# 24 row buffers in the first edge pass of a four-layer graph network, and lookup differences made by TensorE and ScalarE

## The chip, the cores and the metric

The kernel runs on one core of a Trainium2 chip. The metric is the device time of one execution in microseconds (us), smaller is better. The kernel before takes 4315.98 us (median of three runs, 4315.5 to 4325.66).

## The reference, cut to what matters

Four graph layers run one after another over 6250 nodes of 128 features and 100000 edges sorted by destination. The change lies in the first one, an attention layer:

```python
h = jnp.maximum(_layernorm(x, axis=-1), 0.0)
# L0: x + attention(h)
h = x @ W                      # x is the normed h above
a_s = h @ att_src
a_d = h @ att_dst
e = leaky_relu(a_s[src] + a_d[dst], 0.2)
m = segment_max(e, dst)
p = exp(e - m[dst])
denom = segment_sum(p, dst)
out = segment_sum(h[src] * (p / denom[dst])[:, None], dst) + bias
```

Self loops are added to the edges. The sum over edges is taken of the normed rows, and W is applied to the sums per node.

## The kernel before, in words

Nodes are padded to 6656 (52 blocks of 128, 13 groups of 512), edges to 784 tiles of 128, which make 98 chunks of C = 8 tiles. Each phase is a block in which every engine has its own program, and a barrier stands between blocks. The phases of the first layer, with their times in the profiled execution:

- Norm (0 to 43 us): writes the normed rows to the table in HBM and, turned, to `m.hT` in SBUF.
- Setup (`setup_phase`, 43 to 66 us): SyncE loads five index arrays, VectorE splits each source number into its place in a block (`lo`, 7 bits, stored to `lo_dram`) and its block (`m.src_hi`), and makes other constants.
- Tables (`attention_tables_phase`, 66 to 107 us): products of `m.hT` give a_s and a_d; a_s goes through `as_dram`.
- Lookup (`lookup_phase`, 107 to 272 us): finds a_s[src] for every edge, 49 steps of 16 tiles. A step n loads `place` (SyncE, 512 KB, four buffers), compares it with the partition's number (VectorE, `onehot`, L534), multiplies it by a_s in three bf16 parts (PE, 48 products, L559), and takes the entry of the right block: GpSimd subtracts the source's block from the numbers 0 to 51 (`away`, L520), VectorE keeps the product where `away` is zero (`masked`, L540) and sums it up (L546). `onehot`, `away`, `masked` and the PSUM tile have two buffers each.
- Maxima (`segment_max_phase`, 272 to 306 us): scans over the edges on VectorE.
- Edge pass (`attention_edges`, 306 to 1163 us): for each chunk VectorE makes the weights from onehots and ScalarE's exp (`weigh`), PE adds weighted rows and weights into PSUM (L1216, L1217, after a 384-column clear, L788), and VectorE adds them to the accumulator (`add`).
- Output (`attention_output`, from 1163 us): products of the sums and of `m.hT` with W, x loaded again and added.

The rows of the sources are gathered from the table by GpSimd, one indirect DMA of 128 rows (64 KB) for each of the 784 tiles. Since the table stands after the norm, gathers start early: `gather_straight` issues 14 in setup, 30 in tables, one per lookup step, 20 in the maxima, and then what is missing to the ring's end. The ring has RING0 = 16 buffers of 8 tiles, so 128 tiles: `m.rows` (4 buffers) and `m.more` (12). From then on `gather_long_ring` (L838 is the DMA in its helper) waits for `rows_free` of the buffer, and for marks in VectorE's chain. VectorE's loop over chunks has 8 chunks in a turn (SHARED), those of PE and ScalarE have as many as the ring.

## Time and profile before

| what | us |
|---|---|
| median of three runs | 4315.98 |
| the profiled execution | 4312.96 |
| its span, first to last instruction | 4311.2 |
| edge pass of the first layer within it | 306 to 1163 |
| lookup within it | 107 to 272 |

| engine | busy us | share |
|---|---|---|
| PE (matmul) | 3632.9 | 84% |
| PEld (weight load) | 3011.9 | 70% |
| GpSimd | 2880.6 | 67% |
| VectorE | 2142.4 | 50% |
| ScalarE | 1362.6 | 32% |

The shares are averages over four layers with different limits, so they say little about one phase. What matters is read per stage: who is busy, and whom the engine waits for that ends the stage. In the views, "idle before <-releaser" is the time an engine stood still just before an instruction, and what ended it; "issue" is time in which it waited for nothing that the profile shows.

### The profile page before, as it was taken

Reading aid. Unit: us, or ns where it says so; the run is one execution under the profiler, and the core shown is the slowest. Engines: PE = TensorE matmul, PEld = TensorE weight load, DVE = VectorE, ACT = ScalarE, POOL = GpSimd, SP = SyncE. Lnnn points to the kernel's source line nnn. Section 1 sums busy time; section 2 is a strip of 40 time slices with the busy share of each in tenths; the row PEclk is TensorE's granted clock in tenths of the full one; section 3 lists DMA queues with packets and bytes.
Section 4 is the critical chain, followed back from the end, with each engine's and each line's share of the span. In section 5 each row is a group of like instructions: output and inputs, shape, how many; then the busy total and the mean of one; then the engine's idle time right before and its main releaser. Section 6 shows DMA issues by size and latency. Waiting matters only on the chain. (4 is left out here: it accounts for less than half of the span.)

```text
span 4311.2 us, 76764 instructions
## 1 busy us (share of the span) xinstructions
PE 3632.9 (84%) x20596; PEld 3011.9 (70%) x20597; DVE 2142.4 (50%) x6554; ACT 1362.6 (32%) x1910; POOL 2880.6 (67%) x2980
## 2 busy tenths in 40 slices
PE   3649999777678999999998868888888865999997
PEld 1649999767647888888887845555565643777775
DVE  4874444433375555555555744444444446444442
ACT  2000000000051111111113756666666655444442
POOL 4877777777536777777761057777777764777772
PEclk9555555555585555555557978777777775999998
DMA  4632222222263333333322133333333333111122
GB/s 116 200 122 52 53 53 54 53 53 53 71 234 87 79 79 80 77 79 79 79 71 87 51 113 108 105 100 105 100 105 101 104 81 86 52 51 51 50 51 53
DMA packets 257318, 364.29 MB, mean 85 GB/s; under 512 B 53022, under 2 KB 179413, under 8 KB 256981
## 3 DMA queue, kind: packets, MB, share of 16 engines
q0 software_dynamic: 90624, 185.78, 17.0%
q1 hardware_dynamic: 166489, 176.37, 13.3%
q14 instruction: 148, 1.21, 0.1%
q8 instruction: 57, 0.93, 0.1%
HBM read 319.53 MB, written 42.41 MB: 84 GB/s over the span
## 5 line engine op out<-in xcount | busy, mean ns | idle before, releaser
L838 POOL DMA_INDIRECT m_rows<-table,e_idx x1112 | 1065.1, 958 | 350.2 <-issue 291.9
L838 POOL DMA_INDIRECT e_rows<-table,e_idx x480 | 463.2, 965 | 144.7 <-issue 142.6
L838 POOL DMA_INDIRECT m_more<-table,e_idx x480 | 454.0, 946 | 145.6 <-issue 120.4
L1217 PE MATMUL e_agg<-e_weights,m_ones 128*128 128x32 f32 x1568 | 481.6, 401 | 0.0
L838 POOL DMA_INDIRECT m_hT<-table,e_idx x416 | 393.1, 945 | 125.7 <-issue 103.3
L1217 PEld LDWEIGHTS e_agg<-e_weights,m_ones 128*128 128x128 f32 x1568 | 428.3, 333 | 0.0
L1654 PE MATMUL e_z<-e_edge,e_w 128*128 128x512 f32 x392 | 268.3, 822 | 167.2 <-DVEq L1735 153.9
L1216 PE MATMUL e_agg<-e_weights,m_more 128*128 128x16 f32 x1152 | 339.7, 375 | 79.2 <-issue 64.5
L1216 PEld LDWEIGHTS e_agg<-e_weights,m_more 128*128 128x128 f32 x1152 | 311.4, 330 | 105.0 <-issue 105.0
L1543 PE MATMUL e_out<-e_counts,e_nodes 128*128 128x256 bf16 x2964 | 383.2, 280 | 0.0
L1883 PE MATMUL e_x<-e_key,e_rows_T 128*128 x1568 | 373.7, 420 | 2.5 <-DMA e_key<-key_dram 2.5
L1385 ACT ACTIVATE e_counts<-e_count 128x832 bf16<-128x832 f32 x304 | 262.8, 865 | 319.4 <-PE e_count L1536 319.4
L1883 PEld LDWEIGHTS e_x<-e_key,e_rows_T 128*128 128x128 f32 x1568 | 352.5, 330 | 9.5 <-issue 7.6
L1543 PEld LDWEIGHTS e_out<-e_counts,e_nodes 128*128 128x128 bf16 x2964 | 297.8, 101 | 79.5 <-issue 6.2
L1665 PEld LDWEIGHTS e_z<-e_w,e_filt 128*128 128x128 f32 x1568 | 254.2, 254 | 49.0 <-issue 49.0
L1665 PE MATMUL e_z<-e_w,e_filt 128*128 128x128 f32 x1568 | 278.5, 350 | 0.0
L1142 ACT ACTIVATE e_pl<-e_diff 128x8 f32<-128x8 f32 x98 | 20.6, 210 | 802.0 <-DVE e_diff L1176 802.0
L1654 PEld LDWEIGHTS e_z<-e_edge,e_w 128*128 128x128 f32 x392 | 88.3, 250 | 258.1 <-DVEq L1735 157.8
L1844 ACT ACTIVATE e_p<-e_p 128x32 f32<-128x32 f32 x98 | 22.5, 229 | 685.6 <-DVEq L2012 685.6
L1676 PE MATMUL e_agg<-e_onehot,e_message 128*128 128x16 f32 x1568 | 222.1, 285 | 13.2 <-DVE e_message L1747 13.2
L1907 PEld LDWEIGHTS e_agg<-e_weights,m_hT 128*128 128x128 f32 x928 | 199.0, 326 | 42.6 <-issue 42.6
L1676 PEld LDWEIGHTS e_agg<-e_onehot,e_message 128*128 128x128 f32 x1568 | 212.4, 217 | 21.2 <-issue 13.6
(318 smaller groups left out, 6766.2 us busy)
## 6 DMA issues: line engine op xcount, KB each, us to landing
e_edge<-edge_T SPq DMA_DIRECT2D x98, 512.0 KB
lu_place<-lo_dram SPq DMA_DIRECT2D x49, 512.0 KB, 3.8
e_key<-key_dram SPq DMA_DIRECT2D x98, 256.0 KB
m_rows<-table,e_idx POOLq DMA_INDIRECT x1152, 2.6
key_dram<-key_out SPq DMA_DIRECT2D x13, 1024.0 KB, 4.7
table<-m_rows SPq DMA_DIRECT2D x39, 256.0 KB, 2.4
e_rows<-table,e_idx POOLq DMA_INDIRECT x528, 2.6
m_more<-table,e_idx POOLq DMA_INDIRECT x480, 2.5
```

The costliest lines, as they stand in the source:

```text
L838: pool.indirect_dma_start(rows[:, t, :], None, table, bass.IndirectOffsetOnAxis(ap=idx[:, t:t + 1], axis=0)).then_inc(landed[t * len(lande ...
L1142: act.activation(pl[b][:, :, 0], diff[:], ACT.Exp).then_inc(p_ready, 1)
L1216: pe.matmul(to[:, 0, cols], s.rows[at.r][:, t, :], both[:, t, 0, :], start=False, stop=False)
L1217: ins = pe.matmul(to[:, 1:3, cols], m.ones[:], both[:, t, :, :], start=False, stop=(t == C - 1))
L1385: act.activation(counts[at.b][:, :, t * W_NARROW:(t + 1) * W_NARROW].rearrange("p (h n) w -> p h n w", h=2), count_ps[t % 2][:, :, 0:PART] ...
L1543: ins = pe.matmul(out_ps[b][:, 0:L * W_NARROW], nodes[:, part, block_no, :], counts[b][:, block_no, :], start=(i == 0), stop=(i == 3 * NB ...
L1654: ins = pe.matmul(z1[:, cols], w1[:], edge[at.b][:, cols], start=True, stop=True)
L1665: ins = pe.matmul(z2[at.b][:, cols], filt1[at.b][:, cols], w2[:], start=False, stop=(t % G4 == G4 - 1))
L1676: ins = pe.matmul(agg[at.b][:, ds(rel[t], W)], message[at.b][:, t * P:(t + 1) * P], s.onehot[at.b][:, t * W:(t + 1) * W], start=False, sto ...
L1844: act.activation(p[:], p[:], ACT.Exp).then_inc(p_ready, 1)
L1883: ins = pe.matmul(to[:, q * HEADS * W:(q + 1) * HEADS * W], rows_T[:, t, :], key[at.b][:, :, ds(rel[t], W)], start=True, stop=True)
L1907: ins = pe.matmul(to[:, :, ds(rel[t], W)], s.rows[at.r][:, t, :], part[:, q * HEADS * W:(q + 1) * HEADS * W], start=False, stop=(t == C - 1))
```

## The change

The ring of the first edge pass gets 24 buffers: four in `m.rows`, 14 in `m.more` and six (`OVER_HT`) over the first 6144 columns of `m.hT`. For this, the tables phase stores these columns to `hT_dram` in four DMAs of SyncE (`hT_kept`, waited for by GpSimd ahead of tile 128), and the output phase loads them back in four DMAs of ScalarE's queue (`hT_loaded`, waited for by PE's products). The last two buffers of the ring lie in `m.more` and hold `away` during the lookup. The ring's `rows_free` counts are written out for a turn of 24, and each buffer has one semaphore for its eight gathers, not two.

In the lookup, GpSimd no longer makes `away`. PE makes it in two products of 17 rows by 416 columns a step (a row of ones times 0 to 51, less the source's block, from `hi_T`), and ScalarE copies it from PSUM to SBUF. GpSimd issues 17 gathers in 8 steps, not 8 (`lookup_gathers`: 104 in 49 steps, not 49), so 168 tiles are gathered or under way when the edge pass begins, not 113. In setup the load of `src_el` goes, and the block numbers are made from the other array, stored as bf16 (`hi_dram`) and loaded once at the start of the lookup.

```diff
-RING0 = 16
+RING0 = 24
+OVER_HT = 6
...
+def lookup_gathers(step):
+
+    return step * 17 // 8
...
-                sp.dma_start(hi_i[:], k.dram["src_el"]).then_inc(loaded, 16)
...
-                sp.wait_ge(stored, 16)
-                sp.wait_ge(loaded, 80)
+                sp.wait_ge(hi_ready, 1)
+                sp.dma_start(k.dram["hi_dram"].rearrange("(p t) -> p t", p=P), hi_b[:]).then_inc(stored, 16)
+                sp.wait_ge(stored, 32)
+                sp.wait_ge(loaded, 64)
...
-                v.wait_ge(loaded, 80)
...
+                v.wait_ge(loaded, 64)
+
+                ch.step(v.tensor_scalar(hi_i[:], lo_i[:], 7, None, ALU.logical_shift_right))
+                v.tensor_copy(hi_b[:], hi_i[:]).then_inc(hi_ready, 1)
                 ch.step(v.tensor_scalar(lo_i[:], lo_i[:], P - 1, None, ALU.bitwise_and))
                 v.tensor_copy(lo_b[:], lo_i[:]).then_inc(lo_ready, 1)
-                ch.step(v.tensor_scalar(hi_i[:], hi_i[:], 7, None, ALU.logical_shift_right))
-                ch.add(v.tensor_copy(m.src_hi[:], hi_i[:]))
...
                 sp.dma_start(wT[:], k.dram["W0T"]).then_inc(loaded, 16)
...
+                over = OVER_HT * C * P // 4
+                for n in range(4):
+                    sp.dma_start(k.dram["hT_dram"][:, n * over:(n + 1) * over], m.hT[:, n * over:(n + 1) * over]
+                                 ).then_inc(early.hT_kept, 16)
                 sp.wait_ge(copied, NG)
                 sp.dma_start(k.dram["as_dram"].unsqueeze(0), row[:]).then_inc(moved, 16)
                 sp.wait_ge(moved, 16)
...
-        away, masked = [sb(f"away{b}", [P, L, NB], F32) for b in range(2)], [sb(f"masked{b}", [P, L, NB], F32) for b in range(2)]
-        block_ps = [ctx.enter_context(nc.psum_tensor(f"lu_ps{b}", [P, L, PER], F32)) for b in range(2)]
+        masked = [sb(f"masked{b}", [P, L, NB], F32) for b in range(2)]
+        last_rows = (RING0 - RING - OVER_HT - 2) * C * P
+        away = [m.more[:, last_rows + b * L * NB:last_rows + (b + 1) * L * NB].rearrange("p (l n) -> p l n", n=NB) for b in range(2)]
+        assert 2 * L * NB <= 2 * C * P and IN_SETUP + IN_TABLES + lookup_gathers(T // L) <= (RING0 - 2) * C
+        hi_T, away_of = sb("hi_T", [L + 1, T // L, P], BF16), sb("away_of", [L + 1, L, NB], BF16)
+        block_ps, away_ps = [[ctx.enter_context(nc.psum_tensor(f"lu_{n}{b}", [P, L, PER], F32)) for b in range(2)] for n in ("ps", "away")]
...
+        parts = [steps * n // 4 for n in range(5)]
...
+                sp.dma_start(hi_T[1:L + 1, :, :], k.dram["hi_dram"].rearrange("(n t p) -> t n p", t=L, p=P)).then_inc(hi_loaded, 16)
                 for t, d in ((m.dst_here, "dst_el"), (m.dst_beside[:, 0, :], "dst_before"), (m.dst_beside[:, 1, :], "dst_after")):
...
             def _(pool):
                 pool.sem_inc(masked_ready, 2)
...
                     pool.wait_ge(masked_ready, n + 1)
-                    pool.tensor_tensor(away[n % 2][:], m.iota_f[:, 0:NB].unsqueeze(1).to_broadcast([P, L, NB]),
-                                       m.src_hi[:, n * L:(n + 1) * L].unsqueeze(2).to_broadcast([P, L, NB]),
-                                       ALU.subtract).then_inc(away_ready, 1)
-                    gather_straight(pool, k, m, early, k.table[0], IN_SETUP + IN_TABLES + n, 1)
+                    gather_straight(pool, k, m, early, k.table[0], IN_SETUP + IN_TABLES + lookup_gathers(n),
+                                    lookup_gathers(n + 1) - lookup_gathers(n))
...
+            @block.scalar
+            def _(act):
+                for n in range(4):
+                    part = hi_T[0:1, parts[n]:parts[n + 1], :].rearrange("p n d -> p (n d)")
+                    act.activation(part, m.ones[0:1, 0:1].to_broadcast([1, part.shape[1]]), ACT.Copy).then_inc(ones_ready, 1)
+
+                def take(at):
+                    act.wait_ge(numbers_ready, at.n + 1)
+                    act.wait_ge(masked_ready, at.n + 1)
+                    act.activation(away[at.b], away_ps[at.b][:, :, 0:NB], ACT.Copy).then_inc(away_ready, 1)
+                skewed(act, steps, Item, [(0, take)])
...
+                v.tensor_scalar(away_of[:], m.ident[0:L + 1, 1:L + 1].unsqueeze(2).to_broadcast([L + 1, L, NB]), -1.0, None,
+                                ALU.mult).then_inc(away_of_ready, 1)
+                v.wait_ge(away_of_ready, 1)
+                v.tensor_copy(away_of[0:1, :, :], m.iota_f[0:1, 0:NB].unsqueeze(1).to_broadcast([1, L, NB])).then_inc(away_of_ready, 1)
...
-                    v.wait_ge(away_ready, at.n + 1)
+                    v.wait_ge(away_ready, at.n + 3)
...
                 def product(at):
+                    pe.wait_ge(away_ready, at.n + 1)
+                    for half in range(2):
+                        tiles = slice(half * L // 2, (half + 1) * L // 2)
+                        ins = pe.matmul(away_ps[at.b][:, tiles, 0:NB], hi_T[:, ds(at.n, 1), :].rearrange("k n p -> k (n p)"), away_of[:, tiles, :],
+                                        start=True, stop=True)
+                    ins.then_inc(numbers_ready, 1)
                     pe.wait_ge(onehot_ready, at.n + 1)
                     pe.wait_ge(masked_ready, at.n + 1)
                     for q in range(L):
@@ -559,6 +598,10 @@
                             ins = pe.matmul(block_ps[at.b][:, q, 0:NB], onehot[at.b][:, q * P:(q + 1) * P],
                                             m.as_part[:, part, :], start=(part == 0), stop=(part == 2))
...
+                pe.wait_ge(hi_loaded, 16)
+                pe.wait_ge(away_of_ready, 2)
+                pe.wait_ge(ones_ready, 4)
+                pe.sem_inc(away_ready, 2)
                 skewed(pe, steps, Item, [(0, product)])
...
-                gather_straight(pool, k, m, early, k.table[0], IN_SETUP + IN_TABLES + T // (2 * C), IN_MAXIMA)
+                gather_straight(pool, k, m, early, k.table[0], IN_SETUP + IN_TABLES + lookup_gathers(T // (2 * C)), IN_MAXIMA)
...
-    early.gathered = [[nc.alloc_semaphore(f"{name}gathered{r}_{q}") for q in range(2)] for r in range(len(rows))]
+    early.gathered = [[nc.alloc_semaphore(f"{name}gathered{r}")] for r in range(len(rows))]
...
 def gather_straight(pool, k, m, early, table, first, count):
...
+    over_hT = (RING0 - OVER_HT - 2) * C
     for n in range(first, min(first + count, len(early.rows) * C)):
+        if n == over_hT:
+            pool.wait_ge(early.hT_kept, 64)
         pool.indirect_dma_start(early.rows[n // C][:, n % C, :], None, table,
-                                bass.IndirectOffsetOnAxis(ap=m.src_idx[:, n:n + 1], axis=0)).then_inc(early.gathered[n // C][n % C // (C // 2)], 16)
+                                bass.IndirectOffsetOnAxis(ap=m.src_idx[:, n:n + 1], axis=0)).then_inc(early.gathered[n // C][0], 16)
...
-            pool.wait_ge(s.rows_free[r % shared], turn * (ring // shared) + r // shared)
+            pool.wait_ge(s.rows_free[r % shared], (turn - 1) * (ring // shared) + (r // shared + 2))
...
+        over = OVER_HT * C * P // 4
+        hT_loaded = [a.sem(f"hT_loaded{n}") for n in range(4)]
...
                 def products(g):
                     if g >= 3:
                         pe.wait_ge(y_free, g - 2)
+                    if g * GN < 4 * over:
+                        pe.wait_ge(hT_loaded[g * GN // over], 16)
                     for kind, rows in enumerate((acc[:, 0, :], m.hT[:])):
...
             @block.scalar
             def _(act):
+                for n in range(4):
+                    cols = slice(n * over, (n + 1) * over)
+                    act.dma_start(m.hT[:, cols], k.dram["hT_dram"][:, cols]).then_inc(hT_loaded[n], 16)
                 act.wait_ge(shifted, 1)
...
-            m.more = sbuf(layer, "more", [P, (RING0 - RING) * C * P])
-            rows_of = lambda n: m.more[:, n * C * P:(n + 1) * C * P].rearrange("p (t d) -> p t d", d=P)
-            early = early_rows(nc, "g0_", [rows[:] for rows in m.rows] + [rows_of(n) for n in range(RING0 - RING)],
-                               IN_SETUP + IN_TABLES + k.T // (2 * C) + IN_MAXIMA)
+            own = RING0 - RING - OVER_HT
+            m.more = sbuf(layer, "more", [P, own * C * P])
+            rows_of = lambda t, n: t[:, n * C * P:(n + 1) * C * P].rearrange("p (t d) -> p t d", d=P)
+            early = early_rows(nc, "g0_", [rows[:] for rows in m.rows] + [rows_of(m.more, n) for n in range(own - 2)] +
+                               [rows_of(m.hT, n) for n in range(OVER_HT)] + [rows_of(m.more, n) for n in (own - 2, own - 1)],
+                               IN_SETUP + IN_TABLES + lookup_gathers(k.T // (2 * C)) + IN_MAXIMA)
```

## Rows read from the trace of the kernel before

**Rows 1.** By stage: busy us of each engine (instructions), PEclk, DMA share, GB/s

```profile
400.00:500.00 100.00, 97.58 (x437) 92.38 (x437) 46.62 (x250) 4.13 (x15) 75.75 (x82) 0.50 0.21 53
...
900.00:1000.00 100.00, 74.59 (x330) 69.99 (x330) 35.62 (x191) 3.38 (x11) 75.75 (x82) 0.50 0.21 53
```

**Rows 2.** Timeline (start us, us, engine, operation, [idle <-releaser]): gathers

```profile
306.88 0.95 POOL L877 DMA_INDIRECT m_more<-table,m_src_idx  x1 [5.32 <-SPq L1128]
...
328.24 0.97 POOL L838 DMA_INDIRECT m_rows<-table,e_idx  x1 [2.63 <-DVEq L1195]
...
1148.11 0.94 POOL L838 DMA_INDIRECT m_rows<-table,e_idx  x1 [0.30 <-issue]
```

**Rows 3.** Costliest group on GpSimd, 40 to 1160 us

```profile
L838 POOL DMA_INDIRECT m_more<-table,e_idx x480 | 454.0, 946 | 145.6 <-issue 120.4 <-DVE e_masked L1169 7.9 <-DVE e_ade L1171 4.9
```

**Rows 4.** Whom PE waited for (us, times, longest): 400 to 780, 820 to 1140

```profile
PE e_agg L1216 <- DVEq L1185: 14.3, 6, 2.8
...
PE e_agg L1216 <- issue: 72.5, 28, 2.9
```

**Rows 5.** Timeline: chunks 9 and 57 on ScalarE, 57 and 97 on PE

```profile
387.22 0.21 ACT L1142 ACTIVATE e_pl<-e_diff 128x8 f32<-128x8 f32 x1 [11.76 <-DVE e_diff L1176]
...
756.80 0.21 ACT L1142 ACTIVATE e_pl<-e_diff 128x8 f32<-128x8 f32 x1 [12.21 <-DVE e_diff L1176]
...
757.92 0.60 PE L1216 MATMUL e_agg<-e_weights,m_more 128*128 128x16 f32 x2 [2.83 <-DVEq L1185]
...
1152.34 0.60 PE L1216 MATMUL e_agg<-e_weights,m_rows 128*128 128x16 f32 x2 [4.03 <-issue]
```

**Rows 6.** Timeline: one step of the lookup on all engines

```profile
201.96 1.58 POOL L520 TENSOR_TENSOR lu_away<-m_iota_f,m_src_hi 128x832 f32<-128x832 f32 x1 [0.18 <-DVE lu_masked L540]
...
202.04 1.02 DVE L546 TENSOR_REDUCE m_s_el<-lu_masked 128x832 f32 x1 [0.16 <-DVE lu_masked L540]
...
202.97 1.11 DVE L534 TENSOR_SCALAR lu_onehot<-lu_place,m_part_f 128x2048 bf16<-128x2048 bf16 x1
...
203.69 1.24 POOL L877 DMA_INDIRECT m_more<-table,m_src_idx  x1
...
204.01 1.01 DVE L540 SCALAR_TENSOR_TENSOR lu_masked<-lu_away,lu_ps 128x832 f32<-128x832 f32 x1
...
204.15 2.26 PE L559 MATMUL lu_ps<-m_as_part,lu_onehot 128*128 128x52 bf16 x48 [0.88 <-DVE lu_onehot L534]
...
205.10 1.58 POOL L520 TENSOR_TENSOR lu_away<-m_iota_f,m_src_hi 128x832 f32<-128x832 f32 x1 [0.18 <-DVE lu_masked L540]
```

**Rows 7.** Timeline: a onehot of the lookup with GpSimd idle

```profile
117.94 0.75 DVE L534 TENSOR_SCALAR lu_onehot<-lu_place,m_part_f 128x2048 bf16<-128x2048 bf16 x1 [1.13 <-DMA lu_place<-lo_dram]
```

**Rows 8.** Timeline: a scan and the gather begun inside it

```profile
275.32 1.79 DVE L646 TENSOR_TENSOR_SCAN sg_run<-sg_bars,m_s_el 128x784 f32<-128x784 f32 x1
...
275.81 2.06 POOL L877 DMA_INDIRECT m_more<-table,m_src_idx  x1 [0.30 <-issue]
```

**Rows 9.** Groups by form: 384-column product, ScalarE copy of 832

```profile
L788 PE MATMUL e_agg<-m_zeros 1*128 1x384 bf16 x62 | 30.8, 496 | 0.0
...
L1385 ACT ACTIVATE e_counts<-e_count 128x832 bf16<-128x832 f32 x304 | 262.8, 865 | 319.4 <-PE e_count L1536 319.4
```

**Rows 10.** Timeline: first operation of the setup on VectorE

```profile
53.06 0.57 DVE L150 TENSOR_SCALAR su_lo<-su_lo 128x784 int32<-128x784 int32 x1 [10.97 <-DMA su_hi<-src_el]
```

**Rows 11.** Timeline: the last store of the tables phase

```profile
99.31 0.29 SPq L430 DMA_DIRECT2D as_dram<-at_row  x1
```

**Rows 12.** Timeline of the output phase, and its busy time by stage

```profile
1168.60 6.59 SPq L210 DMA_DIRECT2D m_more<-x_in  x4
...
1168.85 2.08 PE L2142 MATMUL o_y<-o_w,m_acc 128*128 128x128 f32 x8 [9.48 <-DMA o_lines<-as_dram]
...
1177.23 15.76 POOL L226 TENSOR_TENSOR m_more<-m_more,o_bias 128x512 f32<-128x512 f32 x11 [28.18 <-DVE o_share L2187]
...
1168.00:1182.00 14.00, 8.45 (x52) 7.94 (x52) 6.44 (x15) 3.61 (x13) 4.77 (x4) 0.74 0.96 250
```

More of the change, by code:

```diff
@@ L118, in setup_phase @@
         hi_i = sb("su_hi", [P, T], I32)
+        hi_b = sb("su_hib", [P, T], BF16)
         span = sb("su_span", [P, 2, T], F32)
@@ L122, in setup_phase @@
         loaded = sem("su_loaded")
-        lo_ready = sem("su_lo_ready")
+        lo_ready, hi_ready = sem("su_lo_ready"), sem("su_hi_ready")
         chain = sem("su_chain")
@@ L494, in lookup_phase @@
         onehot = [sb(f"onehot{b}", [P, L * P], BF16) for b in range(2)]
-        away, masked = [sb(f"away{b}", [P, L, NB], F32) for b in range(2)], [sb(f"masked{b}", [P, L, NB], F32) for b in range(2)]
-        block_ps = [ctx.enter_context(nc.psum_tensor(f"lu_ps{b}", [P, L, PER], F32)) for b in range(2)]
+        masked = [sb(f"masked{b}", [P, L, NB], F32) for b in range(2)]
[4 more added lines that the diff above has]
+        block_ps, away_ps = [[ctx.enter_context(nc.psum_tensor(f"lu_{n}{b}", [P, L, PER], F32)) for b in range(2)] for n in ("ps", "away")]
         place_ready, place_free = [sem(f"place_ready{r}") for r in range(4)], sem("place_free")
-        onehot_ready, block_ready, away_ready = sem("onehot_ready"), sem("block_ready"), sem("away_ready")
+        onehot_ready, block_ready = sem("onehot_ready"), sem("block_ready")
+        hi_loaded, ones_ready, away_of_ready = sem("hi_loaded"), sem("ones_ready"), sem("away_of_ready")
+        numbers_ready, away_ready = sem("numbers_ready"), sem("away_ready")
         masked_ready, picked = sem("masked_ready"), sem("picked")
@@ L537, in pick @@
                     v.wait_ge(block_ready, at.n + 3)
-                    v.wait_ge(away_ready, at.n + 1)
+                    v.wait_ge(away_ready, at.n + 3)
                     v.wait_ge(picked, at.n + 1)
-                    v.scalar_tensor_tensor(masked[at.b][:], away[at.b][:], 0.0, block_ps[at.b][:, :, 0:NB], ALU.is_equal, ALU.mult).then_inc(masked_ready, 1)
+                    v.scalar_tensor_tensor(masked[at.b][:], away[at.b], 0.0, block_ps[at.b][:, :, 0:NB], ALU.is_equal, ALU.mult).then_inc(masked_ready, 1)
                     v.wait_ge(onehot_ready, at.n + 1)
@@ L866, in early_rows @@
     early.rows, early.begun = rows, begun
-    early.gathered = [[nc.alloc_semaphore(f"{name}gathered{r}_{q}") for q in range(2)] for r in range(len(rows))]
+    early.gathered = [[nc.alloc_semaphore(f"{name}gathered{r}")] for r in range(len(rows))]
     early.idx_loaded, early.dst_loaded = nc.alloc_semaphore(name + "idx_loaded"), nc.alloc_semaphore(name + "dst_loaded")
-    early.all = sum(early.gathered, []) + [early.idx_loaded, early.dst_loaded]
+    early.hT_kept = nc.alloc_semaphore(name + "hT_kept")
+    early.all = sum(early.gathered, []) + [early.idx_loaded, early.dst_loaded, early.hT_kept]
     return early
 def gather_straight(pool, k, m, early, table, first, count):
+    over_hT = (RING0 - OVER_HT - 2) * C
     for n in range(first, min(first + count, len(early.rows) * C)):
+        if n == over_hT:
+            pool.wait_ge(early.hT_kept, 64)
         pool.indirect_dma_start(early.rows[n // C][:, n % C, :], None, table,
-                                bass.IndirectOffsetOnAxis(ap=m.src_idx[:, n:n + 1], axis=0)).then_inc(early.gathered[n // C][n % C // (C // 2)], 16)
+                                bass.IndirectOffsetOnAxis(ap=m.src_idx[:, n:n + 1], axis=0)).then_inc(early.gathered[n // C][0], 16)
 def first_turn(pool, k, m, early, table):
@@ L2769, in build @@
                     norm_phase(nc, k, m, "n0_", k.table[0], x_from=k.dram["x_in"], early=early, measured=False)
-                m.src_hi, m.as_part = sbuf(first, "src_hi", [P, k.T]), sbuf(first, "as_part", [P, 3, k.NB], BF16)
+                m.as_part = sbuf(first, "as_part", [P, 3, k.NB], BF16)
                 with ExitStack() as su:
```

4 lines of the change are left out of this document (2 added, 2 removed).

## The prediction

> **What bounds the kernel now.** I went from the stages to the waits, then to single instructions. By stage, the first edge pass has two halves: from 400 to 500 us PE is busy 97.58 of 100 us, from 900 to 1000 only 74.59, while GpSimd stands at 75.6 to 75.8 in both [rows 1]. GpSimd's 75.7% is a full engine: a gather takes 0.946 us, and 0.30 us of idle time follows each (145.6 us over 480) [rows 3]. That makes 1.249 us a tile, 9.99 us a chunk of eight. On the timeline it never pauses: the first gather of the pass starts at 306.88, the first of the loop at 328.24, where it waited 2.63 us for a freed buffer, and the last at 1148.11 [rows 2]. Over 306.88 to 1148.11 stand 671 gathers, the 784 tiles less the 113 before the pass; 670 distances of 1.249 are 836.8 us, the wait and six index copies make up the remaining 4.4 of the 841.2.
>
> PE's waits say the same. From 400 to 780 us it waits only for VectorE's weights, 14.3 us in all; from 820 to 1140 it has 72.5 us in 28 waits at "issue", one ahead of each chunk's products, where the rows aren't there yet [rows 4]. PE lives on the stock of 128 tiles until about 795 us and then walks behind GpSimd. Its own pace is seen on ScalarE's exp, one per chunk: chunk 9 at 387.22, chunk 57 at 756.80 [rows 5], so 369.58 / 48 = 7.70 us a chunk. The pass ends by GpSimd: last gather out at 1149.05, PE starts chunk 97 at 1152.34 [rows 5], 7 us of products, the sums added, and the output phase opens at 1163.6.
>
> GpSimd's whole work is 784 × 1.249 = 979 us from 43 us on, plus what it does besides: 49 differences of 1.58 us. What shortens this layer is each gather that moves from the pass into time in which GpSimd doesn't gather now.
>
> **The change part by part.** *Edge pass.* 168 tiles are issued before it, not 113: 55 gathers fewer, 55 × 1.249 = 68.7 us. With 24 buffers GpSimd goes straight on for 24 gathers (30 us); chunk 0 is freed about 21 us into the pass, as now (wait ended at 328.24, pass began at 306), so the 2.63 us wait goes as well. The marks ask for chunk c - 22 to be weighed; VectorE is there first, now and then. A little longer index copies (192 columns, not 128) cost below 0.5 us. GpSimd's end comes 68.7 + 2.6 - 0.3 = **71.0 us** earlier, and chunk 97 could start at 1081.3.
>
> What is late next is PE. It starts chunk 57 at 757.92 [rows 5]; forty chunks at 7.70 later is 1065.9. So PE is 15 us ahead of GpSimd at the end, catching up with it around chunk 90, and the whole 71.0 counts. It takes 0.16 us more per chunk (15 / 98) before PE binds. The unrolled loops of PE and ScalarE grow from 16 to 24 chunks, which the trace can't price: between a little below 0 (fewer turns) and the 2.83 us that PE waits at a turn of VectorE's loop [rows 5], four times, 11 us. Even this fits into the 15. One semaphore instead of two per buffer changes neither, as PE needs all eight tiles anyway.
>
> *Lookup.* The period of a step is 3.14 us: GpSimd's difference starts at 201.96 and 205.10, and VectorE is full: 1.11 (onehot), 1.01 (masked), 1.02 (sum) [rows 6]. GpSimd is as full, with 1.58 and a gather of 1.24. The onehot takes 0.75 us while GpSimd stands still [rows 7], and 1.11 in this step: it ends at 204.08, 0.54 us after GpSimd's difference (203.54), so it waits for that. Without the difference VectorE needs 0.75 + 1.01 + 1.02 less 0.1 of overlap, 2.7; gathers may hold it up a little, so 2.7 to 3.0. PE now does 48 products in 2.26 us and waits 0.88 for the onehot [rows 6]. It gets two products of 416 columns. Bounds: by the stream of 52-column products, 2.26 / 48 = 0.047 us each or 0.905 ns a column, 2 × 0.38 = 0.75 us; by the lone 384-column product at 0.496 [rows 9], 2 × 0.53 = 1.06 us. They stand ahead of the wait for the onehot, so they fill the 0.88: 2.26 + 0.75 is 3.01, + 1.06 is 3.32. I take 3.05, near the stream, because weights and products follow each other there without a gap. ScalarE's copy of 832 PSUM columns is 0.865 [rows 9], under a 3 us step, and it is over before the 48 products are. GpSimd has 2.125 × 1.249 = 2.65 us a step, 2.95 if each step has one gather stretched by 0.30 as now (1.24 against 0.946), and nobody waits for it inside the phase. So 49 × (3.14 - 3.05) = 4.4 us less. At the start `hi_T` (200 KB in runs of 256 B) goes ahead of the first `place`, about 1 us at the 250 GB/s of [rows 12], and up to 3; the ones (6272 columns on ScalarE, 6.5 us by the 0.865 for 832) and `away_of` (two VectorE operations of 1 us) lie under the wait for the first `place`, 9 us from the phase's start at 107 to the onehot before that of [rows 7]. Lookup: **-3.4 us**, bounds -20 (2.7 a step) to +12 (3.32 a step and 3 us).
>
> *Setup.* VectorE starts at 53.06, when the last of five loads is in [rows 10]. It had stood idle for 10.97 us, so a fifth of the bytes, 401 KB, is at most 2.2 us; the number of VectorE's operations stays. I take **-1.5**, bounds 0 and -2.2. *Tables.* 3.1 MB of stores enter SyncE's queue behind the small loads at 67 us and ahead of the store of a_s at 99.31 [rows 11]. At the 250 GB/s of [rows 12] they are through by 80, so nothing: 19 us of cover. Were it gone, the a_s chain would shift by what is left of them. GpSimd's wait for `hT_kept` stands at tile 128, in the lookup, over 100 us later: nothing.
>
> *Output.* ScalarE's queue loads 3.1 MB from 1164 on. Ahead of the first products stand SyncE's small loads (PE starts at 1168.85), then x is loaded from 1168.60, and GpSimd begins to use it at 1177.23 [rows 12]. The queue moves 250 GB/s in this stretch [rows 12]: 3.1 MB is 12.6 us, 6.5 MB is 26 us from 1164, to 1190. GpSimd adds the bias to 11 groups in 15.76 us, so it asks for the last slab of x (group 9) at 1190, and PE, three groups ahead at most, for the last quarter of `m.hT` no earlier than 1186. So most is covered; the two small round trips ahead of 1173 share the engines with bulk. **+2 us**, bounds 0 and +8.
>
> Sum: -71.0 - 3.4 - 1.5 + 2 = **-73.9 us**. On the profiled execution 4312.96 - 73.9 = 4239.1; this execution lies 3 us below the median of the three runs, so against the median 4315.98 - 73.9 = **4242**.
>
> **Where the Trainium skill speaks against this.** A gather begun inside a VectorE scan takes 2.06 us, not 0.95: the scan started at 275.32 with 1.79 us, and the gather comes out 0.76 us after the scan's end [rows 8]. The Trainium skill, "SBUF — State Buffer", section "SBUF: two separate sides", says that VectorE and GpSimd share one pair of ports under an exclusive lock, and that a GpSimd DMA's descriptors can't be written while VectorE runs in a two-port mode. The trace agrees in kind. By that rule a onehot may shut a gather out for up to its whole length in each step, which is rival A below.
>
> **The rivals.** *A: gathers and onehots collide.* If each of the 2.125 gathers per step is stretched, by 0.30 as now, GpSimd needs 3.29 us a step; with one stretched by 0.75 it is 3.40. Then the lookup ends by GpSimd and costs 49 × 0.2 = 10 us rather than saving 4. For it: the stretched gather is there now. Against: gathers then start at any point of the step, not always inside a onehot. With PE's products at their upper bound the time is about the same: 4242 + 3.4 + 12 = **4257**.
>
> *B: PE runs at its other level in the lookup.* The granted clock is 0.50 (1.2 GHz) in both stretches of the edge pass, even at 97.58% busy [rows 1], and PE in the lookup goes from 72 to some 97% busy. If the clock rose to 1.0, PE's products halve, VectorE alone sets 2.8 a step, and 49 × 0.34 = 17 us are saved, less 1: **4230**. The row of the edge pass speaks against it. The Trainium skill, "TensorE: Matmul & The Clock Gate", section "Part 1: The HAM clock gate", says that the throttled state is the default and sustained activity releases it; that would favour B, but the 97.58% row doesn't agree.
>
> *C: PE is the bound of the pass.* Longer loops or later weights take the chunk to 8.0 us: 40 × 0.3 = 12 behind chunk 57, 17 over the first 57, 29 in all, less the 15 of slack: +14, **4256**. The 16-chunk loops show no stall of PE or GpSimd at their turns, only VectorE's at its 8; against it.
>
> *D: the lookup becomes one chain, the other sign.* `away` now passes PE, ScalarE and VectorE, and PE's wait for `away_ready` stands ahead of the 48 products. If the two buffers don't decouple this, a step is 0.75 + 0.87 + 2.26 + 1.01 and four handovers of some 0.1, 5.3 us: 49 × 2.16 = 106 us more, 4242 + 3.4 + 106 = **4351**, slower. It decides from 3.14 + 71 / 49 = 4.6 us a step. Against it: PE needs only step n - 2's copy, which is over for two whole steps; VectorE needs step n's copy, made under the 48 products.
>
> **How the numbers follow.** Forecast 0.66, range of its own 4232 to 4252 (2.9 to 3.15 a step in the lookup, output 0 to +6, a few us from other layers). A 0.13, B 0.09, C 0.07, D 0.03, and 0.02 for another cause with no gain. The likeliest gives 4242. The range that leaves out D and the tails goes from 4226 to 4263. About 0.3% (13 us) is what a measurement of this kernel can tell from no change; all cases but D and the last are far faster. Faster 0.95, same 0.02, slower 0.03.
>
> **What would show it.** Right: 616 gathers from the start of the edge pass, still 1.249 apart, GpSimd without a wait; PE over 95% busy until near chunk 90 and few waits at "issue" after; the last gather about 71 us nearer to the pass's start. In the lookup, steps of 3.0 to 3.1 us, onehots near 0.8, PE nearly full. Output phase as long as before within 3 us. Wrong would be: PE waiting between chunks in the middle of the pass; a gather waiting for `rows_free`; the pass ended by PE; lookup steps over 3.3; x or `m.hT` late in the output phase, seen as PE's wait for a DMA.

## The result, and the profile after

The kernel after takes 4261.7 us (median of four runs, 4253.4 to 4266.2), the kernel before 4318.7 beside it: ratio 0.9863, 95% interval 0.9851 to 0.9876, so 57 us less by the medians, where 74 were forecast. The profiled execution took 4266.2 us, its span 4263.1; it was the slowest of its four, so the two profiles lie only 46.8 us apart (48.4 by their spans). Phase by phase they differ so:

| phase | forecast | profiles |
|---|---|---|
| setup and tables | -1.5 | -2.0 |
| lookup | -3.4 | -2.8 |
| edge pass, first to last gather | -71.0 | -66.0 |
| output phase | +2 | +8.5 |
| norm and key phases of layer 2 | 0 | +2.9 |
| layer 2's pass | 0 | +6.9 |
| all behind it | 0 | +4.6 |

By stage [rows 1]: PE is now as busy from 900 to 1000 us as it used to be in the first half only, GpSimd at 75.7 as before, and the granted clock stays at 0.50 (1.2 GHz).

```profile
400.00:500.00 100.00, 97.14 (x435) 91.88 (x435) 44.95 (x241) 4.01 (x14) 75.78 (x80) 0.50 0.20 54
900.00:1000.00 100.00, 93.46 (x417) 88.13 (x417) 44.91 (x244) 2.73 (x13) 75.73 (x80) 0.50 0.19 53
```

The gathers of the pass, by the buffer they fill [rows 3]. The mean of one is 951 to 955 ns, not 946:

```profile
L881 POOL DMA_INDIRECT m_more<-table,e_idx x336 | 320.7, 955 | 102.0 <-issue 82.6 <-DVE e_masked L1216 7.0 <-DVE e_weights L1229 4.0
L881 POOL DMA_INDIRECT m_hT<-table,e_idx x144 | 137.0, 951 | 43.9 <-issue 36.0 <-DVE e_onehot L1145 1.8 <-DVE e_masked L1216 1.5
```

Whom PE waited for [rows 4], from 400 to 780 us and from 820 to 1070. The 72.5 us at "issue" are gone; what is left at the end is nine waits for the rows of late chunks (23.1 us; two of the three buffers are shown):

```profile
PE e_agg L1263 <- DVEq L1232: 11.9, 6, 2.3
...
PE e_agg L1263 <- DMA m_hT<-table,e_idx: 15.1, 6, 2.9
PE e_agg L1263 <- DMA m_more<-table,e_idx: 5.3, 2, 2.7
```

The lookup on the timeline [rows 6], first a step with PE at 1.2 GHz, then one at 2.4:

```profile
199.67 0.74 DVE L567 TENSOR_SCALAR lu_onehot<-lu_place,m_part_f 128x2048 bf16<-128x2048 bf16 x1
199.91 0.87 PE L591 MATMUL lu_away<-lu_away_of,lu_hi_T 17*128 17x416 bf16 x2
200.04 1.20 POOL L924 DMA_INDIRECT m_more<-table,m_src_idx  x1 [0.30 <-issue]
...
200.72 2.26 PE L598 MATMUL lu_ps<-m_as_part,lu_onehot 128*128 128x52 bf16 x48
200.82 0.86 ACT L551 ACTIVATE m_more<-lu_away 128x832 f32<-128x832 f32 x1 [3.10 <-PE lu_away L591]
201.48 1.02 DVE L579 TENSOR_REDUCE m_s_el<-lu_masked 128x832 f32 x1
...
204.28 1.02 DVE L579 TENSOR_REDUCE m_s_el<-lu_masked 128x832 f32 x1 [0.16 <-DVE lu_masked L573]
...
205.22 0.52 PE L591 MATMUL lu_away<-lu_away_of,lu_hi_T 17*128 17x416 bf16 x2
...
206.02 1.40 PE L598 MATMUL lu_ps<-m_as_part,lu_onehot 128*128 128x52 bf16 x48 [0.28 <-DVE lu_onehot L567]
...
207.03 1.02 DVE L579 TENSOR_REDUCE m_s_el<-lu_masked 128x832 f32 x1
```

The sums (L579) follow each other after 2.80 and 2.75 us, not 3.14. By this VectorE's part of the lookup, from the phase's start (107.2 before, 105.2 now) to its last sum, went from 164 to 149 us. But the phase is only 2.8 us shorter, and its end shows why:

```profile
253.04 1.02 DVE L579 TENSOR_REDUCE m_s_el<-lu_masked 128x16 f32<-128x832 f32 x1
...
257.51 0.95 POOL L924 DMA_INDIRECT m_hT<-table,m_src_idx  x1 [0.30 <-issue]
267.23 0.33 SPq L641 DMA_DIRECT2D el_dram<-m_s_el  x1
...
267.88 1.21 POOL L924 DMA_INDIRECT m_hT<-table,m_src_idx  x1 [9.42 <-POOLq L522]
```

VectorE is done at 254.1. GpSimd's last gather is out at 258.5, and then nothing is seen for 8.5 us, until the barrier opens at 267.1. GpSimd's program has one drain at the end of each block, the instruction behind which the engine joins the barrier (shortest, median, longest in ns, then when it starts):

```profile
L522 POOLq DRAIN  x1: 18576/18576/18576, 248.4 to 248.4; - x1
```

It ends at 248.4 + 18.6 = 267.0. Nothing else works in the last 6.5 us of it, and no data moves (by stage, the columns of [rows 1]):

```profile
260.50:267.00 6.50, 0.00 (x0) 0.00 (x0) 0.00 (x0) 0.00 (x0) 0.00 (x0) 0.50 0.00 0
```

Before, with 49 gathers in the block, it ended at 264.8 + 7.1 = 271.8, which is 4.1 us past the last gather, and the phase ended 0.6 us after VectorE:

```profile
L503 POOLq DRAIN  x1: 7059/7059/7059, 264.8 to 264.8; - x1
```

The opening of the output phase [rows 12], first two lines of before that the rows do not have, then after:

```profile
1163.64 0.53 SPq L2113 DMA_DIRECT2D line_dram<-m_acc  x2
1175.42 0.29 ACT L2156 ACTIVATE o_e<-o_e 128x104 f32<-128x104 f32 x1 [32.61 <-DVEq L2181]
```

```profile
1092.30 0.54 SPq L2162 DMA_DIRECT2D line_dram<-m_acc  x2
1092.31 2.73 ACTq L2208 DMA_DIRECT2D m_hT<-hT_dram  x4
...
1099.73 0.34 SPq L2167 DMA_DIRECT2D o_lines<-line_dram  x1
1100.11 11.07 SPq L218 DMA_DIRECT2D m_more<-x_in  x4
1105.97 2.08 PE L2193 MATMUL o_y<-o_w,m_acc 128*128 128x128 f32 x8 [17.92 <-DMA o_lines<-as_dram]
...
1112.55 0.29 ACT L2210 ACTIVATE o_e<-o_e 128x104 f32<-128x104 f32 x1 [41.53 <-DVEq L2235]
```

PE's first product comes 13.7 us after the start of the phase, where it was 5.2 (1168.85 less 1163.64), behind SyncE's small load `o_lines`, which was issued at 1094.96 and shares the DMA engines with 3.1 MB issued at 1092.31. ScalarE's exp stands 20.3 us after the start, 11.8 before. From there to ScalarE's last scaled product both kernels take the same 36.5 us.

### The profile page after: what moved, and what is told of

It reads as the page before. It is cut to its first block and busy times, and to the rows that moved or that the text cites. A ratio compares the mean times of both kernels' runs of the same rounds, so it can differ in the third digit from the quotient of the medians.

```text
span 4263.1 us, 76891 instructions
## 1 busy us (share of the span) xinstructions
PE 3642.8 (85%) x20694; PEld 3005.7 (71%) x20695; DVE 2123.1 (50%) x6556; ACT 1407.9 (33%) x1961; POOL 2813.3 (66%) x2929
## 5 line engine op out<-in xcount | busy, mean ns | idle before, releaser
L881 POOL DMA_INDIRECT m_rows<-table,e_idx x1048 | 1006.8, 961 | 329.1 <-issue 291.6
L881 POOL DMA_INDIRECT m_hT<-table,e_idx x560 | 535.0, 955 | 169.6 <-issue 143.2
L881 POOL DMA_INDIRECT m_more<-table,e_idx x336 | 320.7, 955 | 102.0 <-issue 82.6
L1263 PE MATMUL e_agg<-e_weights,m_more 128*128 128x16 f32 x896 | 264.3, 375 | 13.5 <-DVEq L1232 8.2
L1263 PEld LDWEIGHTS e_agg<-e_weights,m_more 128*128 128x128 f32 x896 | 242.2, 330 | 32.4 <-issue 32.4
L1189 ACT ACTIVATE e_pl<-e_diff 128x8 f32<-128x8 f32 x98 | 20.6, 210 | 738.3 <-DVE e_diff L1223 738.3
```

The lines of the kernel that those rows point to most:

```text
L881: pool.indirect_dma_start(rows[:, t, :], None, table, bass.IndirectOffsetOnAxis(ap=idx[:, t:t + 1], axis=0)).then_inc(landed[t * len(lande ...
L1263: pe.matmul(to[:, 0, cols], s.rows[at.r][:, t, :], both[:, t, 0, :], start=False, stop=False)
```

## The experiments

**e1: the kernel before once more.**

> The kernel before, unchanged, with a second profile. In the first two profiles a gather of the first edge pass follows the last after 1.249 us before the change and 1.256 us after it (616 x 0.007 = 4 us), and layers 2 to 4 take 14 us longer after the change, though no line of them differs. Theory 'execution': both are differences of one profiled execution from the next; then this profile's pitch may be either one, and layers 2 to 4 differ from the first profile's by several us. Rival 'kernel': the change causes both (for instance because GpSimd runs no tensor operation in the lookup); then this profile shows 1.249 us again and every phase within 1.5 us of the first one.

4315.1 us, 0.9996 (0.9987 to 1.0006). The gathers of the pass have the pitch and the mean time (946 ns) of the first profile, and layer 2's pass, from the first to the last of ScalarE's 196 operations at L1839, lasts 967.4 us (966.6). But layers 3 and 4 together end 5.9 us earlier than in the first profile with nothing changed: so much of a difference of two profiles means nothing there. What differs in layer 2's pass can be read, what differs in layers 3 and 4 can't.

**e2, e3, e4: the change taken apart.** e2 has the ring, its store and its reload alone; e3 also the new lookup, with one gather a step; e4 has the ring and 104 gathers, with GpSimd making the differences.

```diff
 def lookup_gathers(step):
-    return step * 17 // 8
+    return step
```

(e2 and e3; in e2 and e4 the functions of the lookup and the setup are those of before, the gathers of a step counted by `lookup_gathers`.)

> The ring of 24 buffers with six over m.hT, its store in the tables phase and its load in the output phase, but the lookup and the setup as before: GpSimd makes the differences and issues 49 gathers there, so 113 tiles stand before the pass. Theory 'gathers moved': the ring alone takes away GpSimd's wait of 2.63 us for a freed buffer, and the reload in the output phase costs 8.9 us as in the changed kernel's profile: +6 us against before. Rival 'output cost is due to the earlier phases, not to the reload': -3 us. Rival 'a larger ring helps by itself': below -10 us.

> The changed kernel with one gather per lookup step (49, not 104). Theory 'GpSimd ends the changed lookup': the lookup phase of the changed kernel ended at 267.2 by GpSimd, whose last gather was over at 258.5 and whose drain lasted until 267.0, while VectorE was done at 254.2. With 49 gathers GpSimd keeps pace and its drain is near 4 us as before, so the phase ends near 255 to 257, 16 us earlier than before the change. The pass then has 671 gathers again and takes as long as before less 2.6 us; with +9 in the output phase the whole comes to -5 to -12 us against before. Rival 'the drain belongs to the new lookup, not to the number of gathers': the phase ends near 263 or later, and the whole is 0 to +5 us against before. If the prediction's sum were right (55 gathers are worth 71 us in the pass and cost nothing in the lookup), the whole would be 4242 + 71 = 4313, -3.

> The changed kernel with GpSimd making the differences again, as before, but with the 104 gathers in the lookup. Theory 'GpSimd is the resource': a step of the lookup becomes 1.58 (difference) + 2.125 x 1.25 + 0.2 to 0.5 = 4.4 to 4.7 us instead of 3.14, +62 to +77 us in the lookup and about 4 us more of drain; the pass saves 71 and the output costs 9: +4 to +19 us against before. So the move of the difference to TensorE and ScalarE would be what the gain is made of. Rival 'GpSimd has room': the step stays below 3.6 us and the whole is -35 us or better.

| ratio to before | 49 gathers in the lookup | 104 gathers |
|---|---|---|
| differences by GpSimd | e2: 1.0017 (1.0007 to 1.0026) | e4: 1.0005 (0.9996 to 1.0015) |
| differences by PE and ScalarE | e3: 0.9991 (0.9982 to 1.0001) | after: 0.9863 (0.9851 to 0.9876) |

Against e2, each half alone is worth 0.1 to 0.3% (5 to 11 us), both together 1.5% (66 us). The ring costs 6 us by itself, as expected: its output phase is 8.2 us longer than before, its edge pass 1.0 us shorter.

e4's step is 4.26 us, a little under what was expected:

```profile
203.14 2.24 DVE L545 TENSOR_SCALAR lu_onehot<-lu_place,m_part_f 128x2048 bf16<-128x2048 bf16 x1
203.23 1.60 POOL L530 TENSOR_TENSOR lu_away<-m_iota_f,m_src_hi 128x832 f32<-128x832 f32 x1
204.99 1.24 POOL L892 DMA_INDIRECT m_more<-table,m_src_idx  x1 [0.16 <-issue]
...
206.53 0.94 POOL L892 DMA_INDIRECT m_more<-table,m_src_idx  x1 [0.30 <-issue]
207.40 2.25 DVE L545 TENSOR_SCALAR lu_onehot<-lu_place,m_part_f 128x2048 bf16<-128x2048 bf16 x1
```

The onehot takes 2.24 us where it takes 0.74 otherwise: it begins 0.09 us ahead of GpSimd's difference and ends 0.55 after it, so it stood still for nearly the whole of it. The pass starts 63.4 us later than before, and the 55 gathers give back 69. Against before e4 lost 2 us by the ratio (-2 to +6), where 4 to 19 were expected.

For e3 the lookup was expected to end at 255 to 257; it ends at 251.8, with VectorE:

```profile
246.03 0.95 POOL L924 DMA_INDIRECT m_more<-table,m_src_idx  x1 [1.80 <-DVE lu_masked L573]
...
250.43 1.02 DVE L579 TENSOR_REDUCE m_s_el<-lu_masked 128x16 f32<-128x832 f32 x1
...
252.58 1.21 POOL L924 DMA_INDIRECT m_more<-table,m_src_idx  x1 [5.60 <-POOLq L522]
```

```profile
L522 POOLq DRAIN  x1: 5232/5232/5232, 245.8 to 245.8; - x1
```

The drain is over at 251.0, 4.1 us after the last gather. In e4, with 104 gathers and the old lookup, it is 8.5 us. So in this phase it goes with the number of gathers (49: 4.1, 104: 8.5), not with the kernel. The pass starts 20.6 us earlier than before; of the gain of the 55 gathers (69 us) the changed kernel pays 15 in its lookup. By the whole time e3 gained 4 us, a little less than the 5 to 12 expected, since its pass is 4.3 us longer than before and layer 2's 8.3 us (the gather time, below).

**e5 to e8: on another chip.** In these runs the kernel before took 5542 us.

> The changed kernel, unchanged, as the base for the three below and with a second profile. In e1, e2 and e4 (GpSimd makes the differences) a gather takes 0.94 us and has a pitch of 1.25 from the lookup on to the end of layer 3, and layer 2's pass lasts 966 to 967 us; in the changed kernel and in e3 (TensorE makes them) the gather takes 0.95 with a pitch of 1.26 through layers 1 and 2, and layer 2's pass lasts 974 to 975. Theory 'kernel': this profile repeats 1.26 and 974 (within 1), and the whole is 54 to 60 us below before. Rival 'execution': 1.25 and 966 turn up.

> The changed kernel, but GpSimd doesn't wait for VectorE's step before it issues the gathers of the lookup: 104 of them back to back. In the changed kernel it stands still from 110.7 to 120.6, its last gather is out at 258.5, and its drain ends the phase at 267.0, though VectorE is done at 254.2. Theory 'GpSimd's drain grows with the gathers and ends the phase': the last gather is out near 106 + 104 x 1.33 = 244, the drain of 8.5 us is over at 253, the phase ends with VectorE near 255, and the whole is 12 us (10 to 13) below the changed kernel. Rival 'the drain starts to count only when the phase's other work ends': the phase ends at 263 or later, -4 us at most. Rival 'gathers without pacing collide with VectorE's onehots and the loads of place': VectorE's last step moves past 258, -8 us at most.

> The changed kernel, but in the output phase ScalarE waits until the small line loads are in before it issues the 3.1 MB of m.hT, and TensorE turns the lines ahead of its first product. The opening of the output phase (its start to ScalarE's exp) was 11.8 us before the change and 20.4 after. Theory 'the bulk load stands in the way of the small ones': the opening falls to 11 to 13 us, and the whole by 6 to 9 us below the changed kernel. Rival 'the bytes cost what they cost': m.hT and x come in later instead, PE or GpSimd waits for a DMA further on, and the whole gains less than 3 us.

> The changed kernel with a single GpSimd subtraction more (128 x 208, result unused) at the start of the lookup. Theory 'a tensor operation on GpSimd sets how long the later gathers take': from there the gather takes 0.94 us with a pitch of 1.25, 4 us less in the first edge pass and 7 us less in layer 2's: -11 us against the changed kernel (-8 to -13). Rival 'it isn't the operation' (place of the code, or something else of the old lookup): 0.95 and 1.26 as in the changed kernel, 0 within 2 us.

e6 takes one line away, e7 adds one and moves the transposes, e8 adds one operation:

```diff
                 for n in range(steps):
-                    pool.wait_ge(masked_ready, n + 1)
                     gather_straight(...)
```

```diff
-                products(0)
                 pe.wait_ge(lines_loaded, 64)
...
-                for g in range(1, NG):
+                for g in range(NG):
...
             def _(act):
+                act.wait_ge(lines_loaded, 64)
                 for n in range(4):
```

```diff
+                pool.tensor_tensor(spare[:], m.iota_f[:, 0:NB]..., m.part_f[:]..., ALU.subtract)
```

Against before on the same chip: e5 (the changed kernel) 1.0025 (1.0006 to 1.0043), e6 1.0146 (1.0118 to 1.0174), e7 1.0024 (1.0006 to 1.0041), e8 0.9999 (0.9978 to 1.0020). On this chip the change brings nothing (at best 0.06% slower by its interval), and gathers back to back in the lookup cost 75 us more. The timelines of PE and GpSimd in e6:

```profile
160.61 0.20 PE L597 MATMUL lu_ps<-m_as_part,lu_onehot 128*128 128x52 bf16 x1 [1.90 <-issue]
163.41 0.20 PE L597 MATMUL lu_ps<-m_as_part,lu_onehot 128*128 128x52 bf16 x1 [2.60 <-issue]
166.21 0.20 PE L597 MATMUL lu_ps<-m_as_part,lu_onehot 128*128 128x52 bf16 x1 [2.60 <-issue]
```

```profile
162.28 0.95 POOL L923 DMA_INDIRECT m_more<-table,m_src_idx  x1 [0.30 <-issue]
163.54 0.95 POOL L923 DMA_INDIRECT m_more<-table,m_src_idx  x1 [0.30 <-issue]
```

The gathers keep their pitch, and every other engine stands at "issue": PE shows a product every 2.8 us where 48 took 2.26, and from 160 to 240 us it is busy for 6.4 us, VectorE for 2.7. In e5 VectorE had 60.4 us of "issue" ahead of `e_weights` in the edge pass. There a gather isn't free for the engines beside it, and work moved beside it is paid for. What differs in that chip no trace here shows. The times of these four don't answer the questions they were made for; e6 and e7 were run again. e8's gathers don't bear out its theory either: they kept the long time through the first layer (median 958 ns) and took the short one (947) from layer 2 on.

**e9 and e10, on the first chip.**

> The kernel of e6 once more, since e5 to e8 ran on a chip on which the kernel before took 5542 us, and VectorE and TensorE started an instruction only every 1.4 to 2.7 us while GpSimd gathered. On a chip where before takes about 4318 us: theory 'the drain grows with the gathers and ends the phase': last gather out near 244, drain over near 253, phase over with VectorE near 255, ratio to before 0.9863 - 0.0028 = 0.9835 (0.982 to 0.985). Rival 'the drain counts only from the end of the phase's other work': phase over at 263 or later, 0.9855 or more. Rival 'back-to-back gathers hold the other engines up in the lookup here too, as in e6': the steps of the lookup stretch, phase over after 270, ratio 0.988 or more.

> The kernel of e7 once more, on a chip where before takes about 4318 us. Theory 'the bulk load stands in the way of the small ones': from the start of the output phase to ScalarE's exp 11 to 13 us, not 20.4; ratio to before 0.9863 - 0.0018 = 0.9845 (0.983 to 0.986). Rival 'the bytes cost what they cost': a wait for m.hT or x later in the phase gives it back, and the phase is less than 3 us shorter than in the changed kernel (0.9856 or more).

e9: 4248.9 us, 0.9849 (0.9833 to 0.9866). That is 13 us below the changed kernel by medians but 6 by the ratios to the kernel before beside each, and the two intervals overlap, so the gain is read from the phase. Its lookup ends at 256.8, 10.3 us earlier:

```profile
246.88 1.27 POOL L923 DMA_INDIRECT m_hT<-table,m_src_idx  x1 [0.30 <-issue]
...
250.27 1.02 DVE L578 TENSOR_REDUCE m_s_el<-lu_masked 128x16 f32<-128x832 f32 x1
256.92 0.33 SPq L640 DMA_DIRECT2D el_dram<-m_s_el  x1
```

```profile
L522 POOLq DRAIN  x1: 25117/25117/25117, 231.6 to 231.6; - x1
```

The drain is over at 256.7, 8.5 us after the last gather (248.15), as in the changed kernel: it follows the last gather, whatever VectorE does, and still ends the phase. The gathers that begin inside a onehot (49 of 104) take 1.02 to 1.49 us here too, most of them 1.19, so the last one is 4 us later than expected. No engine starves here as in e6.

e10: 4254.3 us, 0.9858 (0.9842 to 0.9875), which can't be told from the changed kernel; only the phase can be read. The small loads are as quick as before, and half of the gain goes into the wait that the rival named:

```profile
1089.91 0.54 SPq L2162 DMA_DIRECT2D line_dram<-m_acc  x2
...
1094.46 0.34 SPq L2167 DMA_DIRECT2D o_lines<-line_dram  x1
...
1096.52 1.97 ACTq L2208 DMA_DIRECT2D m_hT<-hT_dram  x4
...
1099.47 0.29 ACT L2210 ACTIVATE o_e<-o_e 128x104 f32<-128x104 f32 x1 [30.65 <-DVEq L2235]
...
1104.89 2.07 PE L2193 MATMUL o_y<-o_w,m_acc 128*128 128x128 f32 x8 [7.61 <-DMA m_hT<-hT_dram]
```

The exp comes 9.6 us after the start, not 20.3, but PE's first group needs the first reloaded columns and waits 7.61 us for them, and GpSimd waits 3.55 us for x. From the start of the phase to ScalarE's last scaled product it takes 52.1 us; 48.3 before, 56.8 in the changed kernel. Of the 8.5 us the order of the loads is thus worth 4.7 and the bytes themselves 3.8.

**e11 and e12: on a third chip,** where before took 5470 us. e11 has e9's and e10's edits (with TensorE's first group ahead of the transposes again), and

```diff
-                               [rows_of(m.hT, n) for n in range(OVER_HT)] + ...
+                               [rows_of(m.hT[:, GN:k.NP], n) for n in range(OVER_HT)] + ...
```

> e9's gathers that don't wait for VectorE, and the load of m.hT after the line loads as in e10, but the six buffers lie over columns 512 to 6656 of m.hT, so that the first group of products needs no reload (in e10 ScalarE's exp came 10.6 us earlier against the start of the phase than in the changed kernel, but its first scaled product only 3.0, since TensorE waited for m.hT). Theory 'the two losses are separate and add up': lookup -10.7 as in e9, output phase -7 to -10 against the changed kernel, ratio to before 0.9863 - 0.0025 - 0.0020 = 0.982 (0.980 to 0.9835), 4235 to 4245 us. Rival 'the second and third groups wait instead': output phase -5 at most, ratio 0.9835 or more.

> e11 with one GpSimd subtraction more (128 x 208, result unused) at the start of the lookup. In e8 the gathers turned from 0.95 to 0.94 us at the start of layer 2, in the changed kernel, e9 and e10 only at the end of layer 2, in e1, e2 and e4 in the first layer's lookup. Theory 'the one operation moves the change to the start of layer 2': layer 2's pass 966 to 968 us, not 973 to 975, so 6 to 8 us below e11. Rival 'e8 showed chance': turn at the end of layer 2 as in e9 and e10, within 2 us of e11.

1.0169 (1.0136 to 1.0203) and 1.0141 (1.0107 to 1.0175): as in e6, unpaced gathers starve the lookup. Only the output phase can be read, since GpSimd doesn't gather there: start to exp 11.7 us, and from the start to the last scaled product 50.8 in e11 and 49.5 in e12, which have the same output phase. On e5's chip the same stretch took 56.3 in the changed kernel and 50.7 with e10's edit (e7). The wait has moved to the second group (5.45 us for m.hT), and a gain of the offset beyond e10's edit isn't shown. e12's operation changed nothing clear of noise. The combination was not measured on a chip like the first and stays open.

## Why the prediction came out as it did

The time lies inside the whole range (4226 to 4263) by 1.3 us only, outside the 4232 to 4252 of the likeliest case, and 20 us above its forecast of 4242. The gain came where it was forecast, by the mechanism that was named. Three terms were short: the edge pass by 5.0 us, the output phase by 6.5, and layer 2's pass, put at nothing, by 6.9. In the lookup two larger errors cancelled by luck.

**Edge pass, -71.0: measured -66.0.** The 55 gathers less and the pitch of before account for 55 × 1.252 = 69 us, as written. The wait of 2.63 us for a buffer became one of 0.90 for the index copy (+0.9). The step that failed is "still 1.249": the 615 distances are 1.259 on average without that wait, 0.0075 more than before, 4.6 us. PE's side went as worked out: 7.69 us a chunk, first wait for rows at 989.7, which is chunk 88 ((989.7 - 313.0) / 7.69), where about 90 was forecast. Rival C is out, and the longer loops cost nothing that shows.

**Lookup, -3.4: measured -2.8, but for other reasons.** The step fell by more than forecast. The two 416-column products take 0.87 us at 1.2 GHz, between the two bounds, and the step would be 2.99. But the granted clock was 0.63 on average from 108 to 150 us and 0.73 from 150 to 250; where it stood at the upper level, products and numbers took 1.40 and 0.52, and VectorE alone set 2.75. So the mechanism of rival B, given 0.09, came true in part.

Step by step, the clock rose in stretches where PE's products followed each other without a gap, and fell after steps in which PE waited 0.9 us for the onehot. In the lookup of before, with such a wait in each step, it stayed at 0.50 with PE 72% busy. But in e4's lookup it was 0.53 to 0.54 at 50%, and in the edge pass 0.50 at 97%, so no row here tells what releases it. The Trainium skill, "TensorE: Matmul & The Clock Gate", section "Part 1: The HAM clock gate", has sustained activity release the throttle. That fits the two lookups of before and after, and neither the pass nor e4.

The gain of 15 us was lost again at the end of the phase. The sentence that failed is "nobody waits for it inside the phase": true inside, but the barrier waits for GpSimd, 4.4 us for its gathers and 8.5 for its drain. e3 and e9 show both parts. The two errors cancelled.

Rival A came true in part. A gather that begins inside a onehot ends 0.81 to 0.83 us after that onehot's end, whenever it began (47 of the 104): in the first step above the onehot ends at 200.41, the gather at 201.24. Most began 0.37 us before the onehot's end and so took 1.19 us, not 0.95; together this is 11 us. From 135 to 258 us GpSimd waited for nobody and issued a gather every 1.373 us, 2.92 us a step, more than VectorE's 2.75. So the lookup did end by GpSimd, as A had it, though at 2.92 and not 3.29 to 3.40, and the onehots stayed at 0.74. GpSimd's tensor operation did hold the onehot (2.24 in e4, 1.11 before). The Trainium skill, "SBUF — State Buffer", section "SBUF: two separate sides", has VectorE and GpSimd exclude each other from a shared pair of ports. The traces agree for the tensor operation, and for the gather too: it stood still until the onehot's end. Rival D is out: from 108 to 252 us PE waited once ahead of `lu_away`, at the phase's start, and for onehots 20.2 us, never for ScalarE's copy.

**Setup, -1.5: measured -2.0** by the end of the tables phase. But 1.2 of it is the norm ahead of it, which is unchanged and ended between 40.9 and 42.6 us in the profiles of this chip. VectorE starts 2.8 us sooner after the norm, and GpSimd's drain, now the last to end, takes 2.0 of it back. The store of `m.hT` is hidden, as forecast.

**Output, +2: measured +8.5,** just beyond the bound. The sum asked when the 3.1 MB would be needed, and took the small loads as sharing the engines at little cost. That is the step that failed: everything of the phase stands behind them. The loads ahead of PE's first product were in after 13.7 us, not 5.2, and the exp, which needs the lines stored and loaded again, came after 20.3, not 11.8.

**Other layers, 0: layer 2's pass +6.9.** It is no execution's chance. Measured as in e1, the pass lasts 965.8 to 967.4 us in before, e1, e2 and e4, and 972.8 to 974.9 in after, e3, e9 and e10, and the gathers of layer 2 take 943 to 948 ns in the first four and 955 to 959 in the others. First e1, then after (the buffers in `m.rows`):

```profile
L838 POOL DMA_INDIRECT m_rows<-table,e_idx x284 | 268.4, 945 | 86.5 <-issue 76.5 <-DVE e_top_row L2000 9.7 <-DVE e_col_max L1990 0.3
```

```profile
L881 POOL DMA_INDIRECT m_rows<-table,e_idx x285 | 272.3, 955 | 86.9 <-issue 76.8 <-DVE e_p L2057 4.6 <-PE e_agg L1954 4.3
```

The change thus touches a layer in which no line differs, by the time of a gather; the list at the end has what is known of it.

The five terms sum to -2.0 - 2.8 - 66.0 + 8.5 + 6.9 = -55.4, close to the -57 of the medians. That closeness is partly luck, as the profiles lie 48.4 us apart. Behind the first layer the norm and key phases lost another 2.9 us, 1.5 of which e1 lost too (before has 83.1 us there, every other profile 84.4 to 86.0), so that at the end of layer 2's pass the profiles stand 53.0 apart. The 4.6 us from there to the end are within what e1 shows of chance.

## What to carry to other kernels

Work moved from a full engine to another time pays only where that engine has time until the barrier, its drain included: a sum for a phase needs a line for what each engine does after its last instruction, and gathers belong early in a phase. Neither half of this change is worth much alone; the engine had to be freed and filled at once. A bulk transfer that isn't urgent should be issued behind the small ones whose round trip opens a phase, even on another queue.

## What the runs showed of the hardware that was not expected

- GpSimd's drain at the end of a block goes on after the last gather. In the first layer this time grows with the number of gathers in the block: 14: 2.1 to 2.3 us, 20: 2.3 to 2.6, 30: 2.7 to 3.0, 49: 4.1, 104: 8.5, and 9.2 for 616 and for 671. In the later layers the number alone doesn't give it: 32 gathers have 4.6 to 5.2 us, 480 have 6.0 to 6.3, 752 have 8.6 and 784 have 8.9. It isn't the transfers that it waits for: none moved in its last 6.5 us in the changed lookup. What it waits for is open.
- A gather begun inside a bf16 onehot of VectorE ends 0.81 to 0.83 us after the onehot's end, at whatever point of it the gather began (47 gathers in the changed kernel, 49 in e9, with 0.21 to 0.66 us of the onehot left). Where the gathers fall in the step sets what they cost.
- A gather takes about 0.945 or about 0.955 us (medians), for a whole layer at a time. With GpSimd making the differences it turned to the short time with the lookup, without them at the end of layer 2; with one tensor operation more (e8, e12) at the start of layer 2, while e5 and e11 beside them kept to the end of layer 2. In the last layer it is the other way round: 0.952 to 0.955 in before, e1, e2, e4, e8 and e12, 0.944 to 0.947 in all others. So the operations that GpSimd ran have to do with it, but one of them doesn't turn it at once. The cause is open. It is worth 4.6 us in layer 1 and 7 in layer 2; that e12's operation gains them was not shown, as its chip had layer 2's pass at 1230 us with it and without.
- On two of three chips the kernel before ran 27 to 28% slower. In the changed kernels there the other engines stood at "issue" while GpSimd gathered (e5, e6). On the one of them where the changed kernel itself ran, the change is worth nothing.
